# Router scores of a mixture-of-experts layer: one float32 product against three float16 products of split operands

## The reference

```python
h = jax.nn.relu(jnp.einsum('bsd,hd->bsh', x, Wr1) + br1)     # router, hidden: 192 numbers
score = jnp.einsum('bsd,ed->bse', h, Wr2) + br2              # router, scores of 8 experts
_, idx = jax.lax.top_k(score, 2)
mask = (jax.nn.one_hot(idx, 8) > 0).any(axis=-2)
w = jax.nn.softmax(jnp.where(mask, score, -jnp.inf), axis=-1)
for e in range(8):
    mid = jax.nn.relu(jnp.einsum('bsd,fd->bsf', x, W1[e]) + b1[e])
    out = out + w[..., e:e + 1] * (jnp.einsum('bsf,df->bsd', mid, W2[e]) + b2[e])
```

## Time and profile before

| | |
|---|---|
| time, median of 3 executions | 2048.9 us (2045.86 to 2053.34) |
| span of the profiled execution, first to last instruction | 2041.0 us |
| instructions in it | 54475 |
| PE busy | 1849.8 us, 91% |
| PE weight loads busy | 1378.2 us, 68% |
| DVE busy | 1458.3 us, 71% |
| ACT busy | 1287.1 us, 63% |
| POOL busy | 1139.5 us, 56% |
| DMA, mean over the span | 183 GB/s |

### The profile page before, as it was taken

One profiled execution on the slowest core, in us unless ns is written; L12 is line 12 of the kernel. 1 busy time (PEld: TensorE's weight loads), 2 busy tenths in 40 slices (PEclk: granted clock), 3 DMA queues, 4 the chain that ended last, 5 costly groups with the idle time before them and its releaser, 6 DMA issues. The chain is left out here.

```text
span 2041.0 us, 54475 instructions
## 1 busy us (share of the span) xinstructions
PE 1849.8 (91%) x18013; PEld 1378.2 (68%) x18013; DVE 1458.3 (71%) x4506; ACT 1287.1 (63%) x2661; POOL 1139.5 (56%) x1070
## 2 busy tenths in 40 slices
PE   4898998899889989898898579999999999999996
PEld 4666766666666666666665457777777777767774
DVE  4798889888988898889887456565665655574442
ACT  4688888888888888888888334444444444433332
POOL 4345464645555555555552356766767667664444
PEclk8898999999999999999998569999999999999998
DMA  4586665656566565656554358887888889878985
GB/s 154 147 253 195 186 203 166 196 181 192 174 191 189 179 185 180 194 185 192 174 173 120 102 175 194 197 211 192 199 216 195 198 206 197 198 188 182 187 183 83
DMA packets 362520, 373.10 MB, mean 183 GB/s; under 512 B 144516, under 2 KB 326080, under 8 KB 358272
## 3 DMA queue, kind: packets, MB, share of 16 engines
q1 hardware_dynamic: 320704, 329.03, 55.3%
q0 software_dynamic: 41664, 42.12, 12.3%
HBM read 223.20 MB, written 125.83 MB: 171 GB/s over the span
## 5 line engine op out<-in xcount | busy, mean ns | idle before, releaser
L2021 ACT ACTIVATE mh<-mid_bank 128x512 bf16<-128x512 f32 x336 | 200.6, 597 | 415.2 <-PE mid_bank L1622 415.2
L1923 DVE SCALAR_TENSOR_TENSOR ml<-mid_bank,mh 128x512 bf16<-128x512 f32 x336 | 232.0, 690 | 320.0 <-ACT mh L2021 319.3
L874 DVE TENSOR_REDUCE row_max<-s_bank 98x2 f32<-98x392 f32 x768 | 394.2, 554 | 53.6 <-PE s_bank L650 51.6
L1072 ACT ACTIVATE probs<-t_bank 98x392 f32<-98x392 f32 x768 | 339.7, 499 | 103.9 <-PE t_bank L666 100.5
L2097 POOL DMA_INDIRECT out_rows<-y_out,tail x168 | 267.4, 1592 | 160.7 <-DVE y_out L1957 114.1
L1636 PE MATMUL y_bank<-wst,mh 128*128 128x192 bf16 x1344 | 330.7, 246 | 0.8 <-DVE y_out L1957 0.8
L1639 PE MATMUL y_bank<-wst,ml 128*128 128x192 bf16 x1344 | 330.7, 246 | 0.0
L1638 PE MATMUL y_bank<-wst,mh 128*128 128x192 bf16 x1344 | 330.5, 246 | 0.0
L650 PE MATMUL s_bank<-k_stack,q_stack 96*98 96x196 f16 x1536 | 234.6, 259 | 46.2 <-DVE row_max L874 32.9
L1248 POOL TENSOR_TENSOR x_lo<-x_buf,x_hi 128x588 f16<-128x588 f32 x128 | 170.5, 1344 | 175.1 <-DVE x_b L939 73.0
L666 PE MATMUL t_bank<-q_stack,k_stack 104*98 104x196 f16 x1536 | 225.3, 259 | 32.8 <-ACT probs L1072 29.6
(11 more groups left out here) (257 smaller groups left out, 4527.6 us busy)
## 6 DMA issues: line engine op xcount, KB each, us to landing
wst<-packed SPq DMA_DIRECT2D x56, 1584.0 KB, 8.3
x_buf<-in_x_t SPq DMA_DIRECT2D x32, 1176.0 KB, 7.9
q_stack<-stack_parts SPq DMA_DIRECT2D x288, 98.0 KB, 2.5
k_stack<-stack_parts SPq DMA_DIRECT2D x288, 98.0 KB, 2.6
stack_parts<-qk_hi SPq DMA_DIRECT2D x32, 588.0 KB, 2.9
stack_parts<-qk_lo SPq DMA_DIRECT2D x32, 588.0 KB, 3.1
out_rows<-h_buf SPq DMA_DIRECT2D x32, 294.0 KB
h_in<-out_rows SPq DMA_DIRECT2D x32, 294.0 KB
```

What stands on the lines that cost most here:

```text
L874: nc.vector.reduce_max(row_max[st.odd][:, :, hh:hh + 1], s_bank[hh % 2][0:HALF, :, 0:TOKENS], AX.X).then_inc(max_ready, 1)
L1072: nc.scalar.activation(probs[st.odd][:, hh], t_bank[hh % 2][0:HALF, :, 0:TOKENS], ACT.Exp).then_inc(probs_ready, 1)
L1923: nc.vector.scalar_tensor_tensor(ml[n % MID][:], mid_bank[n % MID_PS][:], 0.0, mh[n % MID][:], ALU.max, ALU.subtract).then_inc(ml_ready, 1)
L2021: nc.scalar.activation(mh[n % MID][:], mid_bank[n % MID_PS][:], ACT.Relu).then_inc(mh_ready, 1)
```

## The change

The scores are computed from float16 parts. The hidden values and the second weight are both kept 1024 times too large, so that the low parts stay in float16's range. ACT writes the relu in float32 as before, without the scale, and then copies it (512 columns in one instruction) to float16 as the high part. DVE subtracts the high part from the float32 values to get the low part (`split_hidden`, new, two instructions of 256 columns), in chunk 2 behind `find_place`. The 192 hidden values are 128 and 64; the second block is laid out twice, so that its high part is in partitions 0 to 63 and its low part in 64 to 127. PE does three float16 products per block: high (128) by the high and low parts of the weight (16 columns), the second block's high and low parts by the same (16 columns), and low (128) by the high part of the weight (8 columns). The two halves of the scores are added by DVE, which takes one more instruction in `route`. `prepare_router` gets six more instructions, and one more small load goes out. The semaphore counts are shifted accordingly (`ROUTE`, `WR1_OPS`, the numbers that `route` and `gap_exponentials` wait for).

```diff
             def prepare_router():
                 nc.vector.memset(router.wr1[:], 0.0).then_inc(wr1_split, 1)
-                nc.vector.memset(router.wr2[1][HI:P], 0.0).then_inc(wr1_split, 1)
+                nc.vector.memset(router.wr2_parts[1][HI:P], 0.0).then_inc(wr1_split, 1)
...
+                nc.vector.tensor_scalar(router.br1[:], router.br1[:], W_SCALE, None, ALU.mult).then_inc(wr1_split, 1)
+                for i in range(2):
+                    nc.vector.tensor_scalar(router.wr2_parts[i][:, 0], router.wr2[i][:], W_SCALE, None, ALU.mult
+                                            ).then_inc(wr1_split, 1)
+                dve.wait_ge(wr1_split, 12)
+                nc.vector.tensor_copy(router.wr1[:, :, DIM:2 * P], router.wr1[:, :, P:DIM]).then_inc(wr1_split, 1)
+                for i, n in enumerate((P, HI)):
+                    nc.vector.scalar_tensor_tensor(router.wr2_parts[i][0:n, 1], router.wr2[i][0:n], W_SCALE,
+                                                   router.wr2_parts[i][0:n, 0], ALU.mult, ALU.subtract
+                                                   ).then_inc(wr1_split, 1)
...
             def router_scores(g):
                 if group_there(g):
-                    pe.wait_ge(rh_ready, 2 * (g + 1))
-                    wait(pe, routed, ROUTE * (g - 1) + 1)
+                    pe.wait_ge(rh_split, 2 * (g + 1))
+                    wait(pe, routed, ROUTE * (g - 1) + 2)
                     wait(pe, placed, PLACE * (g - 1) + 2)
                     for j in range(GTILES):
                         cols = slice(j * P, (j + 1) * P)
-                        nc.tensor.matmul(score_ps[:, j, :], rh[g % 2][:, 0, cols], router.wr2[0][:], start=True,
+                        nc.tensor.matmul(score_ps[:, j], rh_parts[g % 2][:, 0, cols], router.wr2_parts[0][:], start=True,
                                          stop=False)
-                        last = nc.tensor.matmul(score_ps[:, j, :], rh[g % 2][:, 1, cols], router.wr2[1][:], start=False,
-                                                stop=True)
+                        nc.tensor.matmul(score_ps[:, j], rh_parts[g % 2][:, 1, cols], router.wr2_parts[1][:], start=False,
+                                         stop=False)
+                        last = nc.tensor.matmul(score_ps[:, j, 0], rh_parts[g % 2][:, 2, cols], router.wr2_parts[0][:, 0],
+                                                start=False, stop=True)
                     last.then_inc(score_ps_ready, 1)
...
                     dve.wait_ge(score_ps_ready, g + 1)
-                    nc.vector.tensor_tensor(score[:], score_ps, router.br2[:], ALU.add).then_inc(routed, 1)
+                    nc.vector.scalar_tensor_tensor(half_score[:], score_ps[:, :, 1], W_SCALE ** -2, router.br2[:],
+                                                   ALU.mult, ALU.add).then_inc(routed, 1)
                     dve.wait_ge(routed, ROUTE * g + 1)
+                    nc.vector.scalar_tensor_tensor(score[:], score_ps[:, :, 0], W_SCALE ** -2, half_score[:],
+                                                   ALU.mult, ALU.add).then_inc(routed, 1)
+                    dve.wait_ge(routed, ROUTE * g + 2)
...
+            def split_hidden(g):
+                if group_there(g):
+                    q = g % 2
+                    dve.wait_ge(rh_high, g + 1)
+                    wait(dve, score_ps_ready, g - 1)
+                    nc.vector.tensor_tensor(rh_parts[q][:, 2, :], rh[q][:, 0, :], rh_parts[q][:, 0, :], ALU.subtract
+                                            ).then_inc(rh_split, 1)
+                    nc.vector.tensor_tensor(rh_parts[q][HI:P, 1, :], rh[q][HI:P, 1, :], rh_parts[q][HI:P, 1, :],
+                                            ALU.subtract).then_inc(rh_split, 1)
...
                     elif c == 2:
                         find_place(it - 1)
+                        split_hidden(it)
...
             def router_relu(g):
                 if group_there(g):
                     act.wait_ge(r1_ready, g + 1)
+                    wait(act, rh_split, 2 * (g - 1))
+                    for n in range(2):
+                        nc.scalar.activation(rh[g % 2][:, n, :], r_bank[:, n, :], ACT.Relu, bias=router.br1[:, n:n + 1]
+                                             ).then_inc(rh_ready, 1)
+                    act.wait_ge(rh_ready, 2 * (g + 1))
                     wait(act, score_ps_ready, g - 1)
-                    for n in range(2):
-                        nc.scalar.activation(rh[g % 2][:, n, :], r_bank[:, n, :], ACT.Relu, bias=router.br1[:, n:n + 1],
-                                             scale=1.0 / W_SCALE).then_inc(rh_ready, 1)
+                    nc.scalar.copy(rh_parts[g % 2][:, 0:2, :], rh[g % 2][:]).then_inc(rh_high, 1)
```

More of the change, by code:

```diff
@@ L132, in __init__ @@
         self.wr2 = [sb(f"wr2_cols{i}", [P, EXPERTS]) for i in range(2)]
+        self.wr2_parts = [sb(f"wr2_parts{i}", [P, 2, EXPERTS], F16) for i in range(2)]
         self.br2 = sb("br2_rows", [P, GTILES, EXPERTS])
@@ L340, in attention_phase @@
                  (wr1_stage[2][0:HI], wr1_a[HI:P]), (wr1_stage[2][HI:P], wr1_b), (router.br1[:], br1),
-                 (router.wr2[0][:], wr2_a), (router.wr2[1][0:HI], wr2_b), (router.br2[:], br2),
+                 (router.wr2[0][:], wr2_a), (router.wr2[1][0:HI], wr2_b), (router.wr2[1][HI:P], wr2_b),
+                 (router.br2[:], br2),
                  (router.ids[:], expert_ids)]
-        WR1_OPS = 9
+        WR1_OPS = 15
         BIAS_OPS = 12
@@ L1352, in expert_phase @@
         rh = [sb(f"rh{i}", [P, 2, GT]) for i in range(2)]
+        rh_parts = [sb(f"rh_parts{i}", [P, 3, GT], F16) for i in range(2)]
+        half_score = sb("half_score", [P, GTILES, EXPERTS])
         score = sb("score", [P, GTILES, EXPERTS])
@@ L1443, in expert_phase @@
         small_bank = ps("small_bank", [P, 512])
-        score_ps = small_bank[:, 0:GTILES * EXPERTS].rearrange("p (j e) -> p j e", j=GTILES)
+        score_ps = small_bank[:, 0:2 * GTILES * EXPERTS].rearrange("p (j s e) -> p j s e", j=GTILES, s=2)
         spare_ps = small_bank[:, 384:384 + EXPERTS * TJ].rearrange("p (e j) -> p e j", e=EXPERTS)
@@ L1456, in expert_phase @@
         rh_ready = sem("rh_ready")
+        rh_high = sem("rh_high")
+        rh_split = sem("rh_split")
         score_ps_ready = sem("score_ps_ready")
@@ L1483, in expert_phase @@
         CONSTS = 5
-        ROUTE = 10
+        ROUTE = 11
         GATES = 4
@@ L1698, in route @@
                         nc.vector.max_index(top_at[:, j, :], top[:, j, :], score[:, j, :]).then_inc(routed, 1)
-                    dve.wait_ge(routed, ROUTE * g + 6)
+                    dve.wait_ge(routed, ROUTE * g + 7)
                     nc.vector.tensor_copy(top_id[:], top_at[:, :, 0:2]).then_inc(routed, 1)
@@ L1703, in route @@
                                           ).then_inc(routed, 1)
-                    dve.wait_ge(routed, ROUTE * g + 7)
+                    dve.wait_ge(routed, ROUTE * g + 8)
                     shape = [P, GTILES, 2, EXPERTS]
@@ L1707, in route @@
                                             top_id[:].unsqueeze(3).to_broadcast(shape), ALU.is_equal).then_inc(routed, 1)
-                    dve.wait_ge(routed, ROUTE * g + 9)
+                    dve.wait_ge(routed, ROUTE * g + 10)
                     wait(dve, place_ps_ready, g - 1)
@@ L2006, in gap_exponentials @@
                     q = g % 2
-                    act.wait_ge(routed, ROUTE * g + 4)
+                    act.wait_ge(routed, ROUTE * g + 5)
                     wait(act, gates_ready, GATES * (g - 1))
```

2 lines of the change are left out of this document (1 added, 1 removed).

## The result

The changed kernel takes 2037.1 us (median of 4 runs, 2034.0 to 2040.2) against 2051.1 for the kernel before on the same chip (4 runs, 2045.9 to 2054.2). The ratio is 0.9939, with a 95% interval from 0.9917 to 0.9961: by it a gain of 12.5 us (the medians lie 14.0 apart), where 23.8 were forecast. The time lies just above the forecast's range (2037.14 against 2037.0). The recorded texts call the engines TensorE (PE), VectorE (DVE), ScalarE (ACT), GpSimd (POOL) and SyncE (SP).

What follows compares the result with a forecast made beforehand. PE was taken to bound the 39 iterations with tile and group, POOL the groups without tiles. -25.7 (scores) + 1.0 (groups without tiles) + 0.9 (preparation) = -23.8 us: span 2017.2, median 2025.1 us; range 2019 to 2037.

Steps and rivals of the forecast that it cites:

- The scores on PE: Each group's scores: six float16 products take 0.15 us instead of 0.81, gaining 0.66 us a group, 25.7 us over 39.
- The forecast of 549.5 us between tiles 0 and 38: Among the tiles: ends of tiles 0 and 38 lie 38 x 14.46 = 549.5 us apart, instead of 574.6.
- Copy and split among the tiles: Among the tiles: ACT's copy (0.61 us) and DVE's subtractions (0.40 each) fit idle gaps, cost 0.
- The other rounds among the tiles, cost 0: Among the tiles: POOL, token loads and DMA (share 0.87) keep up with PE's 14.46 us round, cost 0.
- DMA is the bound: Rival, among the tiles: transfers can't go faster, the round stays at 15.12 us, kernel 2051 us; chance 0.04.
- Groups without tiles, +1.0: Before the first tile: POOL's sends bound the round at 5.11 us; subtractions holding up its transfers cost 1.0 us.
- eight rounds of POOL and a landing: What lies between the first send (1157.81) and the first tile's transposed load (1201.58).
- The forecast's 4.9 us for the round at the low clock: Groups without tiles: the round of PE, ACT and DVE goes from 4.96 to 4.9 us, under POOL's 5.11.
- the 3 us that I had named as the sign of a wrong prediction: Start of the first tile: the prediction is wrong if it comes over 3 us later.
- The last 17 tiles "gain nothing": The last 17 tiles have no scores, so they gain nothing.
- two chunks away: Among the tiles: if the next tile's token load were late, the tile needing it would still be two chunks away.
- Preparation, +0.9: `prepare_router`: six small DVE instructions added while PE waits behind it, cost 0.9 us, ends 0 and 1.5.

Runs made afterwards that it cites:

- the five buffers: Changed kernel with five buffers instead of three for each tile's small load (gates and token numbers): 2024.7 us, ratio 0.9892; repeated, 2029.2 us, ratio 0.9899.
- the kernel with the high part only: Changed kernel with ACT writing the relu as float16, without copy and subtractions, the hidden values' low part left out of the scores: 2029.0 us, ratio 0.9904.
- the second comparison: Both kernels, unchanged, profiled a second time beside each other: before 2050.9 us, changed 2039.7 us, ratio 0.9942.

## Why the prediction was wrong

**The scores on PE: right.** 0.15 us for six products, no wait in front of them, a tile round of 14.47 us for the 14.46 forecast. The forecast of 549.5 us between tiles 0 and 38 became 551.5. The 2 us more are nearly all three longer rounds (14.72, 15.74, 14.68).

**Copy and split among the tiles: right.** The copy took 0.62 us (forecast 0.61), each subtraction 0.42 (0.40), hidden, as the kernel with float32 products and the split shows.

**The other rounds among the tiles, cost 0: off by 1.7 us.** One of the longer rounds, where PE waited 1.10 us at a tile's first product, and ACT for the tokens (changed kernel):

```profile
1339.19 0.38 PE L1634 MATMUL mid_bank<-xT,wst 128*128 128x512 f16 x1 [1.10 <-issue]
...
1339.12 0.62 ACT L2052 COPY xe<-xT 64x512 f16<-64x512 f16 x1 [1.40 <-DMA xT<-slots]
```

At a round of 15.13 us no profile had a longer round; at 14.47 each profile had one to six, at other tiles each time. What delays the loads in these rounds is not shown. The rival "DMA is the bound" may be right for this small part.

**Groups without tiles, +1.0: the step that failed first.** I named POOL as the bound by its round of 5.11 us ("eight rounds of POOL and a landing"). The rounds are still 5.11 us (5.3 where a subtraction hits a send) and the eighth group's last send starts only 0.4 to 0.6 us later. What I had wrong is the landing: I took it as fixed, but these sends land beside the first weight load, and that one waits for DVE's `select`. The length of DVE's own round I never summed. The forecast's 4.9 us for the round at the low clock was right (4.97); missing were the rounds in which the clock is at its full level, where the kernel before gained and DVE's bound doesn't let the changed one gain, and the split that stands ahead of `select`. The weight load went out 3.5 and 3.0 us later and with it the token load, 3.5 and 3.1; tile 0's first product came 2.6 and 2.7 us later (the 3 us that I had named as the sign of a wrong prediction lie between), its end 2.1 us later on average. Since one of the 39 groups with a gain lies before that end, the term measured 2.1 + 0.66 = 2.8 us instead of 1.0.

The price that I did put there, subtractions holding up POOL's transfers, exists. One hit costs the 0.2 us that I took for it, but there are only one or two in the eight rounds, 0.2 to 0.4 us instead of 0.9:

```profile
1186.86 1.18 POOL L2118 DMA_INDIRECT slots<-row_r,spot  x1 [0.17 <-issue]
```

```profile
1186.76 0.42 DVE L1742 TENSOR_TENSOR rh_parts<-rh,rh_parts 64x256 f16<-64x256 f32 x1
```

The send started 0.10 us into the subtraction and took 1.18 us instead of 0.96 to 0.99. In the first ten groups of all profiles with the split (the very first send, 1.21 us in every kernel, left out), sends that started 0.05 to 0.10 us into a subtraction took 1.15 to 1.22 us, those at 0.14 to 0.23 us 1.04 to 1.11, and those within its first 0.04 us or after 0.28 us the usual time; in the four profiles of kernels without the split no send behind the first took over 0.99. On this the Trainium skill ("SBUF — State Buffer", "Who interferes with whom") says that a tensor_tensor had not been seen to stall descriptors; the traces don't agree, neither for these short subtractions nor for the 1.22 us instruction of the earlier trace rows.

**The last 17 tiles "gain nothing": the step that cost most.** They lost 4.8 us on PE and 1.4 us at the end. I had said of the loads that the next tile would be "two chunks away", and had looked at their order only among the groups. In the last tiles PE's round is 12.78 us and the loop of adds, small load and weight load needs 13 to 14; the changed kernel enters that stage with less lead (its weight loads go out 34.1 us before the end of tile 38 instead of 36.0), and its adds lag by 10 us six tiles sooner. That the loop takes the time is shown by the five buffers; that the smaller lead is why it takes more here is argued, and can't be all of it: the kernel with the high part only had the same lead (34.3) and lost 1.1 us instead of 4.8.

**Preparation, +0.9: the size fits.** From its first instruction to the row maxima behind it DVE takes 2.80 us instead of 2.15 in both pairs of profiles, and PE's wait there is 2.16 us instead of the 1.50 of the earlier trace rows:

```profile
126.49 1.03 PE L652 MATMUL s_bank<-k_stack,q_stack 96*98 96x196 f16 x4 [2.16 <-DVE row_max L886]
```

So it costs 0.66 us at its place. The times of the attention phase alone can't tell that from nothing.

**The sum.** With the measured terms: -25.5 (one round before the end of tile 0, 37 whole ones of 0.655 and the last, which is only 0.56 shorter) + 1.7 + 2.8 + 4.8 + 1.4 = -14.8, the 14.7 us that the two pairs of profiles show for the expert phase; +0.7 for the preparation makes 14.1. The terms are read from the same profiles, so that they add up is no second proof, and 2.8 and 1.4 are uncertain by the 1 to 3 us by which profiles of the kernel before differ there. The medians say 14.0 and, in the second comparison, 11.2 (2050.9 - 2039.7); the first ratio's interval reaches from 8 to 17 us.

## What to carry to other kernels

When a stage's bound gets shorter, look at the stages that the change does not touch: a loop there that runs on its stored lead (a buffer freed by a late write, a load behind it on the same queue) may just have held, and the gain is given back after the last edit's reach. For each stage, sum the round of every engine and queue at both levels of the clock, and follow the load that starts the next stage back to the wait that ended last, and that wait to whatever its transfer lands beside, instead of choosing the engine whose round looks longest. A deeper buffer for a small load, here five instead of three, may be worth more than half as much as the edit itself (10 us against 14).

## What the runs showed of the hardware

A float32 product with 8 columns and a new stationary operand took 0.10 us per record at the full clock, a float16 one with 8 or 16 columns 0.025 us. In the groups without tiles the granted clock stayed mostly at its lower level (1.2 GHz; the mean was 0.54 from 1160 to 1200 us in the changed kernel, with PE busy for 64% of it, and 0.55 in the kernel before with 84%), and three products of 512 columns more per round brought it to the full one (2.4 GHz) from 20 to 47 us after the start. Small indirect sends of POOL landed 2.4 us after their issue when alone, and 3.5 to 6.3 us after it when issued during a weight load of 7.1 us, about when that load landed. A send started 0.05 to 0.23 us into a 0.42 us subtraction of DVE took up to 1.22 us instead of 0.96 to 0.99. The attention phase, in which these kernels differ only in the preparation, ended between 1144.7 and 1161.3 us in their profiles, with falls of the clock at other places each time; I don't know what places them.
